# A state-space megakernel: where z is projected and its silu taken, and one buffer for dtx

## The reference

```python
def _mamba(u, in_w, conv_w, conv_b, xp_w, dt_w, dt_b, A_log, Dp, out_w):
    x, z = jnp.split(u @ in_w.T, 2, axis=-1)             # 512 + 512 channels
    xc = conv_b + sum(xpad[:, k:k + L, :] * conv_w[:, k] for k in range(4))
    x = silu(xc)
    xdbl = x @ xp_w.T                                    # dt rank 16, B 16, C 16
    dt = softplus(xdbl[..., :16] @ dt_w.T + dt_b)
    dA = exp(dt[..., None] * A)
    dBx = (dt * x)[..., None] * B[:, :, None, :]
    h = dA * h + dBx                                     # scan over time, 16 states
    y = sum_n(h * C) + x * Dp
    return (y * silu(z)) @ out_w.T
```

## Time and profile before

| | us |
|---|---|
| median of 3 runs | 6042.82 (6040.0 to 6043.99) |
| the profiled execution | 6041.77, span 6040.0 |
| TensorE busy (share of the span) | 5095.7 (84%) |
| VectorE busy | 5052.4 (84%) |
| ScalarE busy | 3549.0 (59%) |
| GpSimd busy | 5066.3 (84%) |
| mean granted clock of TensorE | 0.903 |
| dbx on GpSimd, 1792 times | 3695.0, 2090 ns each |
| scans on VectorE, 1232 + 560 times | 2483.2 + 1128.6, about 2016 ns each |
| first scan of the first and of the second mamba | at 377.94 and 3095.46 |

### The profile page before, as it was taken

One profiled execution on the slowest core, in us unless ns is written; L12 is line 12 of the kernel. 1 busy time (PEld: TensorE's weight loads), 2 busy tenths in 40 slices (PEclk: granted clock), 3 DMA queues, 4 the chain that ended last, 5 costly groups with the idle time before them and its releaser, 6 DMA issues. The chain is left out here.

```text
span 6040.0 us, 69966 instructions
## 1 busy us (share of the span) xinstructions
PE 5095.7 (84%) x25566; PEld 3554.5 (59%) x25566; DVE 5052.4 (84%) x3473; ACT 3549.0 (59%) x5494; POOL 5066.3 (84%) x2582
## 2 busy tenths in 40 slices
PE   6968888888888888888678888888888888888789
PEld 5836565665565566555545566655665566665544
DVE  3459999999999999999949999999999999999900
ACT  0046666666666666666546666666666666666511
POOL 0059999999999999999859999999999999999900
PEclk8988989989989989999889998899988999899789
DMA  4123223233232332323123313132231322313164
GB/s 153 70 101 100 94 76 108 68 98 100 71 108 68 99 100 70 108 68 98 59 76 100 104 66 107 64 103 90 80 108 62 104 82 87 108 62 101 56 212 143
DMA packets 220108, 563.74 MB, mean 93 GB/s; under 512 B 27794, under 2 KB 94226, under 8 KB 218228
## 3 DMA queue, kind: packets, MB, share of 16 engines
q1 hardware_dynamic: 203956, 532.52, 27.1%
q10 hardware_dynamic: 15808, 26.75, 1.2%
HBM read 499.06 MB, written 60.13 MB: 93 GB/s over the span
## 5 line engine op out<-in xcount | busy, mean ns | idle before, releaser
L868 POOL TENSOR_TENSOR dbx<-dtx,b_all 128x896 f32<-128x896 f32 x1792 | 3695.0, 2090 | 0.2
L708 ACT ACTIVATE mamba_ps<-dt,w 128x448 f32<-128x448 f32 x3584 | 2132.4, 629 | 1555.9 <-DVE hc L820 1288.7
L813 DVE TENSOR_TENSOR_SCAN mamba_ps<-mamba_ps,dbx 128x896 f32<-128x896 f32 x1232 | 2483.2, 2016 | 211.0 <-ACT mamba_ps L708 109.7
L661 PEld LDWEIGHTS mamba_ps<-ident,hc 128*112 128x112 f32 x14336 | 1782.6, 145 | 787.9 <-issue 390.3
L661 PE MATMUL mamba_ps<-ident,hc 128*112 128x128 f32 x14336 | 2043.7, 295 | 234.3 <-POOL hc L875 141.9
L820 DVE TENSOR_TENSOR hc<-mamba_ps,c_all 128x896 f32<-128x896 f32 x1232 | 1341.6, 1089 | 137.1 <-DVE mamba_ps L813 3.4
L875 POOL TENSOR_TENSOR hc<-hc,c_all 128x896 f32<-128x896 f32 x560 | 1166.7, 2083 | 226.0 <-DVE hc L813 223.5
L813 DVE TENSOR_TENSOR_SCAN hc<-mamba_ps,dbx 128x896 f32<-128x896 f32 x560 | 1128.6, 2015 | 117.9 <-ACT mamba_ps L708 117.9
L577 PE MATMUL mamba_ps<-u,w 128*128 128x448 f32 x1792 | 880.6, 621 | 387.7 <-DVE sz L802 298.3
L577 PEld LDWEIGHTS mamba_ps<-u,w 128*128 128x128 f32 x1792 | 337.9, 209 | 643.2 <-DVE sz L802 327.3
L586 PE MATMUL mamba_ps<-x,taps 128*128 128x448 f32 (+3 forms) x1792 | 704.5, 536 | 12.0 <-ACT x L722 12.0
(11 more groups left out here) (101 smaller groups left out, 2863.6 us busy)
## 6 DMA issues: line engine op xcount, KB each, us to landing
b_all<-bc_scratch SPq DMA_DIRECT2D x448, 448.0 KB, 5.8
c_all<-bc_scratch SPq DMA_DIRECT2D x448, 448.0 KB, 5.1
u<-u_scratch SPq DMA_DIRECT2D x56, 448.0 KB, 7.7
y_scratch<-ytok SPq DMA_DIRECT2D x56, 448.0 KB, 3.2
src<-y_scratch SPq DMA_DIRECT2D x56, 448.0 KB, 4.6
xb<-in_x SPq DMA_DIRECT2D x4, 3136.0 KB, 11.6
u_scratch<-ub ACTq DMA_DIRECT2D x28, 448.0 KB, 8.2
src<-in_x SPq DMA_DIRECT2D x28, 448.0 KB, 6.8
```

The source lines that it names most:

```text
L661: ins = nc.tensor.matmul(y_ps[j % 2][:, c * 128:(c + 1) * 128], hc[g][:, e * T + c * TCH:e * T + (c + 1) * TCH], ident[:, :], start=False, ...
L708: ins = nc.scalar.activation(decay[g % 2][:, e * T:(e + 1) * T], blk(dt[t % 2], j), ACT.Exp, scale=w[:, c:c + 1])
L813: nc.vector.tensor_tensor_scan(dst, h, dbx[n % BX_RING][:, :], 0.0, ALU.mult, ALU.add).then_inc(scan_done, 1)
L868: nc.gpsimd.tensor_tensor(view(dbx[n % BX_RING], 0, [[T, 2], [1, T]]), view(dtx[t % 2], j * T, [[0, 2], [1, T]]), view(b_all, 2 * g * T, [ ...
```

## The change

z leaves `FRONT`. It is projected for the own tile in slots 0, 1, 4 and 5, so the items x and c of the next tile move back. The session of z moves from slot 3 to slot 8. ScalarE's copy of out1 moves from slot 16 to slot 15, its copy of y3's sum from 3 to 4, y2 on TensorE from 30 to 29. dtx has one buffer where it had two, and a wait for its own last readers on GpSimd. SyncE now loads u of the tile after next once z3 of the own tile is projected. The lines of the table:

```diff
 SCHEDULE = {
-    "x0": (0, 1), "x1": (1, 2), "c0": (3, 5), "c1": (4, 6), "y3": (6, None), "x2": (7, 8), "x3": (9, 10), "c2": (10, 11),
...
+    "z0": (0, 1), "z1": (1, 2), "x0": (2, 3), "x1": (3, 4), "z2": (4, 5), "z3": (5, 6), "c0": (6, 7), "y3": (6, None),
+    "c1": (8, 9), "x2": (8, 10), "x3": (10, 11), "c2": (10, 12), "c3": (12, 13), "out0": (13, 14), "out1": (15, 15),
...
-SILU_Z_AT, SILU_X_AT, SOFTPLUS_AT = 3, 16, 24
-TAKE_Y_AT = {3: 3, 12: 0, 20: 1, 28: 2}
+SILU_Z_AT, SILU_X_AT, SOFTPLUS_AT = 8, 16, 24
+TAKE_Y_AT = {4: 3, 12: 0, 20: 1, 28: 2}
```

Besides the table:

```diff
-FRONT = ("x0", "x1", "c0", "c1", "x2", "x3", "c2", "c3", "xp", "dt0", "dt1", "dt2", "dt3", "z0", "z1", "z2", "z3")
+FRONT = ("x0", "x1", "c0", "c1", "x2", "x3", "c2", "c3", "xp", "dt0", "dt1", "dt2", "dt3")
-        dtx = [sb(f"dtx{p}", DB * T) for p in range(2)]
+        dtx = sb("dtx", DB * T)
-                        sp.wait_ge(work_ready, Item(t, FRONT[-1]).ready())
+                        sp.wait_ge(work_ready, Item(t, "z3").ready())
                         load_u(t + 2)
...
+                            elif name[0] == "z":
+                                in_proj(t, name, DIN + int(name[1]) * 128)
                             else:
                                 turn_back(t, int(name[1]))
...
+                def take_z(t, j):
+                    it = Item(t, f"z{j}")
+                    nc.scalar.copy(blk(sz[t % 2], j), take(it)[:, 0:T]).then_inc(work_free[it.slot], 1)
...
+                            elif name[0] == "z":
+                                take_z(t, int(name[1]))
...
+                        upto(pool, dbx_ready, SLOTS * (t - 1) + 16 * (h + 1))
                         ins = nc.gpsimd.tensor_tensor(dx, d, pair(x[t % 2], h), ALU.mult)
```

More of the change, by code:

```diff
@@ L614, in front_item @@
                         conv(t, int(name[1]))
-                    elif name[0] == "z":
-                        in_proj(t, name, DIN + int(name[1]) * 128)
                     else:
@@ L725, in take_front @@
                                              bias=w[:, W_CB + j:W_CB + j + 1]).then_inc(work_free[it.slot], 1)
-                    elif name[0] == "z":
-                        nc.scalar.copy(blk(sz[t % 2], j), take(it)[:, 0:T]).then_inc(work_free[it.slot], 1)
                     else:
                         nc.scalar.copy(blk(dt[t % 2], j), take(it)[:, 0:T]).then_inc(work_free[it.slot], 1)
+                def take_z(t, j):
+                    it = Item(t, f"z{j}")
+                    nc.scalar.copy(blk(sz[t % 2], j), take(it)[:, 0:T]).then_inc(work_free[it.slot], 1)
                 def silu_x(t):
@@ L851, in make_dtx @@
                     h = k // 2
-                    d, dx = pair(dt[t % 2], h), pair(dtx[t % 2], h)
+                    d, dx = pair(dt[t % 2], h), pair(dtx, h)
                     if k % 2 == 0:
                         pool.wait_ge(softplus_ready, t + 1)
+                        upto(pool, dbx_ready, SLOTS * (t - 1) + 16 * (h + 1))
                         ins = nc.gpsimd.tensor_tensor(dx, d, pair(x[t % 2], h), ALU.mult)
@@ L867, in make_dbx @@
                     upto(pool, scan_done, n + 1 - BX_RING)
-                    nc.gpsimd.tensor_tensor(view(dbx[n % BX_RING], 0, [[T, 2], [1, T]]), view(dtx[t % 2], j * T, [[0, 2], [1, T]]),
+                    nc.gpsimd.tensor_tensor(view(dbx[n % BX_RING], 0, [[T, 2], [1, T]]), view(dtx, j * T, [[0, 2], [1, T]]),
                                             view(b_all, 2 * g * T, [[T, 2], [1, T]]), ALU.mult).then_inc(dbx_ready, 1)
```

## The result

The changed kernel takes 6189.77 us (median of 4 runs, 6185.64 to 6198.97), the kernel before 6041.41 in the same comparison: ratio 1.0244, 95% interval 1.0226 to 1.0261, slower by 148 us. The forecast was 6210, the range 6045 to 6280. The profiled execution (6198.97, span 6196.9) is the slowest of the four, 157 us above that of before. One run in this document, of the changed kernel with out1 in slot 17, took 7952 us at a mean granted clock of 0.58; the ratios leave it out.

What follows compares the result with a forecast made beforehand. VectorE's scans waited 227.6 us for ScalarE's decays, with TensorE late mid-tile and GpSimd the next wall. 52 tiles x (2.5 + 1.1) = +187, last tiles -2, first -1, starts -15.7: +168 on 6041.8 gives 6210 us, range 6045 to 6280.

Steps and rivals of the forecast that it cites:

- The queue and the hand-off: Slots 0 to 17: z items delay TensorE, x3 waits for c1's copy, scans 15 to 17 start late; +2.5 us a tile.
- the case that was slower still: Rival, chance 0.08: z1, x0, x1 and z2 all at half clock, z copied late, scan 9 waits some 2.3 us; 6330 us.
- the dt stretch: Slots 19 to 25: half clock on TensorE raises waits from 2.1 to 3.2 us; +1.1 a tile, bounds 0 and 2.1.
- The starts: Start of each mamba: four projections and copies leave, so softplus comes 7.85 us earlier; -15.7 us for both.
- The first tiles: First tile of each mamba: no out0 and out1 in TensorE's queue; -1 us together.
- dtx: GpSimd's wait before writing the single buffer is already met, last reads some 13 slots or more earlier; 0 to 0.04 us.
- last tiles: Last tile of each mamba: the wait at scan 4 goes and nothing comes; -2 us together.
- The faster case: Rival, chance 0.13: TensorE not late, out1's copy starts at 43.8, scan 17 doesn't wait, GpSimd is the floor; 5920 us.
- The equal case: Rival, chance 0.07: scans 15 to 17 stall, but full clock in slots 19 to 25 cuts waits to 0.2; 6054 us.

## Why the prediction was right

**The queue and the hand-off.** The path through a tile came out as worked: decays 9 at 24.04 (24.07 forecast), x3 at 25.84 (25.8), out1's copy at 45.76 (45.65), scan 15 at 42.33 (42.3), scan 16 at 47.48 (47.5), scan 17 at 52.99 (53.0). A tile takes 3.10 us more; less the 0.55 of the dt stretch (next paragraph) that leaves 2.55 for what was forecast at 2.5. Of the case that was slower still only its beginning came: z1 ran at half clock (3.34 us), the projection behind it at full (1.67). That the hand-off of c1's bank places x3 was argued there and is shown by the run with half of z. That the copy in slot 15 turns TensorE's lateness into waits of VectorE is shown by moving it alone, both ways.

**The dt stretch** was mis-sized: taken 3.2 with bounds 2.1 to 4.2, measured 2.65, so +0.55 us a tile instead of +1.1. It is the term of the sum that was too large. The long kind of gap before xp (1.77 us) came in all 52 tiles, and half clock came with it in 49 of them; so far the reason given holds. What it left out is how long half clock lasts. In 33 tiles it lasts through the four dt items (14.7 us instead of 7.8), and scan 25 waits 1.98. In 14 it ends on the way (10.8 us), and scan 25 waits 0.41; in 2 it costs nothing. So the mean stayed near the lower bound, 2.1. And a long gap before xp is not enough by itself: with 3.24 us of it the dt items run at full clock if nothing idles before dt0. That the clock makes these waits is shown by the matmuls before dt0.

**The starts** brought 3.5 us in the first mamba and 7.3 in the second, not 15.7 together. In the first, TensorE ran xp and the dt items at half clock, so the copies that softplus waits for came late themselves:

```profile
366.10 0.53 ACT L727 COPY dt<-mamba_ps 128x448 f32<-128x448 f32 x1 [0.96 <-PE mamba_ps L603]
366.65 1.28 ACT L742 ACT_TABLE_LOAD   x1
```

Softplus does start right behind the last dt copy, as forecast (366.65 after a copy of 0.53 at 366.10), but only 3.5 us before its old time. The first tiles, forecast at -1, cost +6.4 and +1.5: c1 is not ready there when ScalarE wants it (in the first mamba this convolution takes 5.25 us instead of 3.09), and scans 9 and 10 wait up to 1.13 and 2.21.

```profile
404.03 0.63 ACT L724 ACTIVATE x<-mamba_ps,w 128x448 f32<-128x448 f32 x1 [3.75 <-PE mamba_ps L586]
```

**dtx.** That one buffer costs nothing was right. But the distance of "13 slots or more" holds for the first pair of blocks only. The second is written in slot 6, 7 slots after its last reader in slot 31 of the tile before.

**The sum.** In the profiled executions 52 tiles x 3.10 = +161.2, first tiles +7.9, starts -10.9, last tiles -1.6, what follows the mambas +0.3: +156.9, all that was measured, against 187 - 1 - 15.7 - 2 = 168 forecast. The error is mostly the dt stretch, 52 x 0.5 = 26 us too much. The first tiles (9 too little) and the starts (5 too little) set off half of it, which was luck. By the medians the forecast is 20 us too high, since the profiled execution is 9 us above the median of the four.

**The rivals.** The faster case did not come: out1's copy started at 45.8, not before 43.8. The run with out1 in slot 17 shows that even with TensorE as late as here the waits can go: it is 200 us below the kernel before, more than the 123 of that case. The equal case (full clock in the dt stretch) did not come by itself either. The run with matmuls before dt0 brings it about: 6054 measured, 6054 worked out. That they agree to the us is luck, since the first tiles cost 6 us there too, where -1 was put.

## What to carry to other kernels

In an engine that works in order, an instruction that may wait belongs behind the one that others need next, not ahead of it. When a queue gets longer, look at every consumer of it that stands ahead of critical work. The value of an edit should be read with such a place mended: here a table that looked 2.4% worse was 3.3% better with one number different. Then compare it with the old table mended in the same way: out1 in slot 17 brings 2.4% there, and with the session of z in slot 8 and x2 copied a slot earlier the old table comes to 0.9682 against 0.9667, which the intervals don't tell apart. So what the change brought seems to be the place of a session; that z is projected for the own tile shows no gain of its own. And when work takes turns in two banks, follow who empties the bank: that, more than the sum of the work, says when an item starts.

## What was not expected of the hardware

TensorE's clock in a light stretch decides over VectorE. At 1.2 GHz a dt item with its sums takes 3.67 us instead of 1.96, which is more than the 2.8 us of a slot, and the copies that ScalarE has in its list wait for it. Three matmuls of no use, 2.26 us in a gap of 2.57, took 131 to 136 us from two kernels. The gap directly before the light items is the one to close. In the six kernels that idle 2.57 us before dt0, half clock came somewhere in the dt stretch in 33 to 51 of the 52 tiles; in the six in which the gap is 0.14 to 0.32 us, in none, though TensorE idled up to 4.3 us before xp. Among the first six, how often half clock comes and how long it stays differs, and no run here isolates what decides it.
